# Cross-attention and mixture of experts on one core: the normed queries' rows of batches two to eight are turned on VectorE and placed by DMA instead of transposed on TensorE

## The reference, cut to what matters

```python
def xattn(query, key, value, Wq, Wk, Wv, Wo):      # 16 heads of 16
    q = (query @ Wq.T).reshape(B, L, H, D) * D ** -0.5
    k = (key @ Wk.T).reshape(B, -1, H, D)
    v = (value @ Wv.T).reshape(B, -1, H, D)
    scores = sigmoid(einsum('blhd,bshd->bhls', q, k))
    return einsum('bhls,bshd->blhd', scores, v).reshape(B, L, E) @ Wo.T

x = x + xattn(layernorm(x), ctx, ctx, Wq, Wk, Wv, Wo)
x = x + moe(layernorm(x), gate_w, Wg, Wu, Wd, Ws_g, Ws_u, Ws_d)   # top-64 tokens per expert and batch
```

## Time and profile before

| what | value |
|---|---|
| median of three runs | 1366.16 us |
| the profiled execution | 1361.12 us, of which the span of its instructions is 1359.3 us |
| TensorE matmul busy | 1320.3 us (97%) |
| ScalarE busy | 981.3 us (72%) |
| VectorE busy | 631.8 us (46%) |
| GpSimd busy | 283.5 us (21%) |
| granted TensorE clock, mean | 0.998 |

### The profile page before, as it was taken

How to read it: one execution, slowest core, us unless ns; L and a number is a source line. 1 busy time by engine, 2 the same in 40 slices (tenths; PEclk the granted TensorE clock), 3 DMA queues, 4 the chain that set the end, 5 groups by cost and what they waited for, 6 DMA issues and landing times.

```text
span 1359.3 us, 22554 instructions
## 1 busy us (share of the span) xinstructions
PE 1320.3 (97%) x8834; PEld 755.1 (56%) x8834; DVE 631.8 (46%) x1249; ACT 981.3 (72%) x1137; POOL 283.5 (21%) x286
## 2 busy tenths in 40 slices
PE   4899999999999999999999999999999999999997
PEld 3444344444444444444444443324888888888886
DVE  4353254235226335423522531211658777777762
ACT  3568988888888888888888889997232445555553
POOL 1000020002002002000200200220000466777645
PEclk9999999999999999999999999999999999999999
DMA  6466784587388478458738836833433567877754
GB/s 162 137 142 154 126 161 138 114 143 192 104 138 181 143 116 171 138 115 143 190 104 140 184 105 92 144 126 109 156 124 124 186 191 177 200 191 190 185 109 47
DMA packets 119433, 196.85 MB, mean 145 GB/s; under 512 B 22752, under 2 KB 71904, under 8 KB 119328
## 3 DMA queue, kind: packets, MB, share of 16 engines
q1 hardware_dynamic: 99456, 161.44, 50.0%
q0 software_dynamic: 19584, 33.59, 12.7%
q10 hardware_dynamic: 288, 0.39, 0.2%
HBM read 118.99 MB, written 61.83 MB: 133 GB/s over the span
## 4 chain that ended last, share of the span: by engine, by line
PE 89%; ACT 5%; DVE 2%; issue 1%; SPq 1%; DMA 1%; POOL 0%; POOLq 0%; DVEq 0%; ACTq 0%
PE acc L1420 25%; PE score L1458 19%; PE score L1396 18%; PE score L1476 9%; PE misc L1304 6%; PE misc L1317 6%; ACT probs L735 5%; PE misc L1340 2%; PE misc L1325 2%; SPq L471 1%; PE misc L1332 1%; DMA keys<-key_parts 0%; PE misc L1355 0%; DMA xn<-x 0%; DVE key_parts L851 0%
## 5 line engine op out<-in xcount | busy, mean ns | idle before, releaser
L735 ACT ACTIVATE probs<-score 128x1024 f32<-128x1024 f32 (+1 forms) x832 | 788.6, 1041 | 131.3 <-PE score L1396 125.1
L1420 PE MATMUL acc<-probs,values 128*32 128x512 f32 (+1 forms) x3328 | 412.4, 600 | 1.4 <-ACT probs L735 0.4
L1396 PE MATMUL score<-queries,keys 48*128 48x512 f32 (+1 forms) x1664 | 311.6, 448 | 4.1 <-DMA keys<-key_parts 2.9
L1396 PEld LDWEIGHTS score<-queries,keys 48*128 48x128 f32 (+1 forms) x1664 | 126.7, 180 | 261.1 <-ACT probs L735 200.4
L1420 PEld LDWEIGHTS acc<-probs,values 128*32 128x32 f32 (+1 forms) x3328 | 81.0, 108 | 181.6 <-issue 135.4
L618 POOL DMA_DIRECT2D ctx_raw<-ctx_t x32 | 23.4, 732 | 684.0 <-DVE ctx_lo L840 683.2
L744 ACT ACTIVATE gelu<-score 128x512 f32<-128x512 f32 x96 | 56.6, 599 | 96.5 <-PE score L1458 95.0
L678 POOL DMA_INDIRECT gathered<-norm_scr,gather_row x64 | 80.8, 1262 | 204.5 <-DVE gather_row L1116 189.3
L1458 PE MATMUL score<-tok_hi,gu_hi 128*128 128x512 f32 x384 | 119.2, 391 | 0.0
L1458 PE MATMUL score<-tok_lo,gu_hi 128*128 128x512 f32 x384 | 118.5, 390 | 0.0
L1458 PE MATMUL score<-tok_hi,gu_lo 128*128 128x512 f32 x384 | 118.3, 389 | 0.0
(11 more groups left out here) (185 smaller groups left out, 1430.3 us busy)
## 6 DMA issues: line engine op xcount, KB each, us to landing
keys<-key_scr SPq DMA_DIRECT2D x180, 200.2 KB, 9.2
key_scr<-key_parts SPq DMA_DIRECT2D x45, 512.0 KB, 5.0
gu_raw<-w_gu SPq DMA_DIRECT2D x17, 1024.0 KB
ctx_raw<-ctx_t POOLq DMA_DIRECT2D x24, 512.0 KB, 4.2
queries<-query_scr SPq DMA_DIRECT2D x180, 64.0 KB, 2.8
d_raw<-w_d SPq DMA_DIRECT2D x17, 512.0 KB
query_scr<-query_parts SPq DMA_DIRECT2D x15, 512.0 KB, 4.8
norm<-xn SPq DMA_DIRECT2D x224, 32.0 KB
```

The lines of the kernel that those rows point to most:

```text
L735: act.activation(probs[0:rows, n % RING, 2 * pair:2 * pair + 2, :], score[k % 3][0:rows, :, :], ACT.Sigmoid, scale=SCALE).then_inc(probs_d ...
L1396: mm = pe.matmul(score[k % 3][0:rows, g, :], keys[quarter % KEY_RING][of, pair, P * st:P * st + rows], queries[half][of, e, pair, :], star ...
L1420: mm = pe.matmul(acc[32 * c:32 * (c + 1), :], values[b % 2][0:rows, st, half, c, :], probs[0:rows, n % RING, c, :], start=(st == 0), stop= ...
```

## The change

The T products of batches 1 to 7 go. Their rows take the way of the second norm: `turn_x` (one STREAM_TRANSPOSE of `xn` into `norm_blocks`, at quad 26, in batch 0 at quad 21), `place_x` (16 DMAs of 32 KB on GpSimd's queue, back into the bytes of `xn`), `split_x` (four VectorE instructions at quad 33, in batch 0 at quad 31). Q waits for that split. In batches 1 to 6 of the loop Q(c, 0) is at quad 38 where it was at 31, K(c, 0, 3) and K(c, 1, 3) at 40 and 41 (41 and 43), V(c, 3, 0) at 44 (45); most other products move by a quad or two. Batch 0 of the input keeps its two T products ahead of the loop. SP's load of the x rows of the batch after moves from the second T to Q(c, 0), behind a wait for the split.

The plan of sums follows from the list. Quads of a batch b = 1 to 6, by their number of sums: before 21 with none, 21 with two, 10 with one; after 19, 19 and 14. Batch 0: before 21, 19 and 12; after 22, 20 and 10. Batch 7 has no product but O, O and G in both, O at 5 and 8 where they were at 4 and 7.

```diff
 def beside(b):
     if b == 0:
...
-        at_quad = (13, 14, 16, 18, 19, 21, 23, 25, 26, 28, 30, 32, 33, 35, 37, 39, 40, 42, 44)
+        at_quad = (13, 14, 16, 18, 20, 22, 24, 26, 28, 30, 32, 34, 36, 38, 39, 41, 44)
     else:
-        tasks = {4: ("O", b - 1, 0), 7: ("O", b - 1, 1), 26: ("G", b - 1)}
-        at_quad = (0, 2, 10, 13, 15, 18, 21, 24, 28, 29, 31, 33, 35, 37, 39, 41, 43, 45, 47)
+        tasks = {5: ("O", b - 1, 0), 8: ("O", b - 1, 1), 26: ("G", b - 1)}
+        at_quad = (0, 2, 10, 12, 15, 17, 20, 24, 28, 30, 32, 34, 38, 40, 41, 44, 47)
     if b + 1 < B:
         c = b + 1
         names = [("K", c, 0, 0), ("K", c, 1, 0), ("V", c, 0, 0), ("V", c, 0, 1),
                  ("K", c, 0, 1), ("K", c, 1, 1), ("V", c, 1, 0), ("V", c, 1, 1),
-                 ("T", c, 0), ("T", c, 1), ("Q", c, 0),
-                 ("K", c, 0, 2), ("K", c, 1, 2), ("V", c, 2, 0), ("V", c, 2, 1),
+                 ("K", c, 0, 2), ("K", c, 1, 2), ("V", c, 2, 0), ("V", c, 2, 1), ("Q", c, 0),
                  ("K", c, 0, 3), ("K", c, 1, 3), ("V", c, 3, 0), ("Q", c, 1)]
...
             def load_x(b):
-                sp.wait_ge(misc_copied, COUNT["T", b - 1, KC - 1])
+                if b == 1:
+                    sp.wait_ge(misc_copied, COUNT["T", 0, KC - 1])
+                else:
+                    sp.wait_ge(x_split, b - 1)
                 sp.dma_start(xn[:], x_rows[b]).then_inc(x_in, 16)
...
                         elif task[0] == "Q":
+                            if task[2] == 0 and task[1] + 1 < B:
+                                load_x(task[1] + 1)
                             write_queries(*task[1:])
                             if task[1] and task[2] == 0:
                                 stack_queries(task[1], 0)
-                        elif task[0] == "T" and task[2] == KC - 1 and task[1] + 1 < B:
-                            load_x(task[1] + 1)
...
+            def place_x(b):
+                pool.wait_ge(x_turned, b)
+                place_blocks(x_raw, x_placed)
+
+            for kc in range(NCH):
+                load_ctx(1, kc)
+            place_x(1)
+            for b in range(2, B):
+                load_ctx(b, 0)
+                if b >= 3:
+                    place_x(b - 1)
+                for kc in range(1, NCH):
                     load_ctx(b, kc)
-                if b >= 2:
-                    place_norm(b - 2)
+                place_norm(b - 2)
+            place_x(B - 1)
             place_norm(B - 2)
...
+            def turn_rows(of, turned_one):
+
+                dve.transpose(norm_blocks.rearrange("p j (t q) -> p t j q", q=TURN),
+                              of[:].rearrange("p t (j q) -> p t j q", q=TURN)).then_inc(turned_one, 1)
...
+            def turn_x(b):
+                dve.wait_ge(xn_ready, b + 1)
+                wait_past(dve, nt_stored, STORE * (b - 1))
+                turn_rows(xn, x_turned)
...
+            def split_x(b):
+                dve.wait_ge(x_placed, PLACE_DMAS * b)
+                split_rows(x_raw, x_split)
...
-                    if kind == "T" and k == 0:
-                        wait_past(dve, nt_stored, STORE * (b - 1))
...
-                    if b and q == 7:
+                    if b and q == 8:
                         second_sums(b - 1)
...
+                    if b + 1 < B and q == (21 if b == 0 else 26):
+                        turn_x(b + 1)
+                    if b + 1 < B and q == (31 if b == 0 else 33):
+                        split_x(b + 1)
...
                 elif kind == "Q":
+                    if task[2] == 0:
+                        wait_past(pe, x_split, b)
                     mm = query_product(task[2], bank)
```

More of the change, by code:

```diff
@@ L282, in build @@
         tok_raw = norm[:].rearrange("p t d -> p (t d)").rearrange("p (k s) -> p k s", s=S)
+        x_raw = xn[:].rearrange("p t d -> p (t d)").rearrange("p (k s) -> p k s", s=S)
         last_out = logits[:].rearrange("p t b e -> p (t b e)")[:, 0:P]
@@ L317, in build @@
         norm_ready = sem("norm_ready")
+        x_turned = sem("x_turned")
+        x_placed = sem("x_placed")
+        x_split = sem("x_split")
         norm_turned = sem("norm_turned")
@@ L635, in _, with place_blocks @@
                 load_ctx(0, kc)
+            def place_blocks(to, placed_one):
+                for i in range(BLOCKS):
+                    for j in range(BLOCKS):
+                        pool.dma_start(to[TURN * j:TURN * (j + 1), :, P * i:P * (i + 1)],
+                                       norm_blocks[TURN * i:TURN * (i + 1), j::BLOCKS, :]).then_inc(placed_one, 16)
             def place_norm(b):
@@ L639, in place_norm @@
                 pool.wait_ge(norm_turned, b + 1)
[L640 to L646, removed]
+                place_blocks(tok_raw, norm_placed)
+            def place_x(b):
[9 more added lines that the diff above has]
+                for kc in range(1, NCH):
                     load_ctx(b, kc)
-                if b >= 2:
-                    place_norm(b - 2)
+                place_norm(b - 2)
+            place_x(B - 1)
             place_norm(B - 2)
@@ L954, in second_sums, with split_rows @@
                 norm_sums(resid)
+            def turn_rows(of, turned_one):
+                dve.transpose(norm_blocks.rearrange("p j (t q) -> p t j q", q=TURN),
+                              of[:].rearrange("p t (j q) -> p t j q", q=TURN)).then_inc(turned_one, 1)
             def turn_norm(b):
                 dve.wait_ge(norm_ready, b + 1)
[L958 to L962, removed]
+                turn_rows(norm, norm_turned)
+            def turn_x(b):
+                dve.wait_ge(xn_ready, b + 1)
+                wait_past(dve, nt_stored, STORE * (b - 1))
+                turn_rows(xn, x_turned)
+            def split_rows(placed_raw, split_one):
                 for k in range(KC):
[L964 removed]
+                    raw = placed_raw[:, k, :].rearrange("p (i t q) -> p t i q", i=BLOCKS, q=TURN)
                     hi = nt_hi[:, k, :].rearrange("p (t i q) -> p t i q", i=BLOCKS, q=TURN)
@@ L969, in split_norm @@
                     last = dve.tensor_tensor(lo, raw, hi.bitcast(F32), ALU.subtract)
-                last.then_inc(norm_split, 1)
+                last.then_inc(split_one, 1)
+            def split_norm(b):
+                dve.wait_ge(norm_placed, PLACE_DMAS * (b + 1))
+                split_rows(tok_raw, norm_split)
+            def split_x(b):
+                dve.wait_ge(x_placed, PLACE_DMAS * b)
+                split_rows(x_raw, x_split)
             def gate_logits(b):
```

## The result

The changed kernel takes 1376.11 us, the median of 5 runs (1372.26 to 1377.15). The kernel before took 1366.16 us on the same chip. The ratio is 1.0071, 95% interval 1.0050 to 1.0091: 10 us slower, where 7.5 us faster was forecast. What happened is the second rival, the late keys, with a second cost behind it that no rival had priced: TensorE's clock.

What follows compares the result with a forecast made beforehand. TensorE was taken to bound the kernel, working through its list almost without waiting; 5.9 us from batches 1 to 6 plus 1.6 from batch 0 gave 1366.2 - 7.5 = 1358.7 us, range 1355.5 to 1364.5.

Steps and rivals of the forecast that it cites:

- the second rival: First score of batches 2 to 7: keys land late, costing six times the excess over 0.7 us; 1373 us; chance 0.10.
- The price of the list: TensorE in batches 1 to 6: its quads priced start to start, each batch going from 113.0 to 112.0 us.
- two pairs lost: Sums in batches 1 to 6: two pairs become four singles, losing 0.32 us of the 1.30 gained per batch.
- batch 0: Batch 0: two T products gone, one pair of sums more, a wait behind the second T; 1.6 us gained.
- The first rival: Runs of short quads in each batch: ScalarE takes back up to 0.5 us a batch; 1361.7 us; chance 0.12.
- The placing of x: GpSimd's 16 DMAs after quad 26: landing 3.1 to 8.7 us after issue, 4.4 us of cover at worst; nothing reaches TensorE.
- the third rival: GpSimd's queue, six batches: each of 16 placing DMAs held 1.8 us, 130 us slower; decides from four to five holds; chance 0.02.
- the cost is taken at zero: SP's queue behind the later Q(c, 0): no cost, or 0.3 us a batch if the landing is 1 us later.
- the margin of 0.7 us: Batch end: the sixth key DMA lands 0.7 us before the new quarter starts, where it was 1.5.
- The key writes: SP's queue behind the query stack: small writes taking 0.5 us each to issue and landing in 1.8 us.
- The query write and its stack: SP's queue after quad 38: queries written at 702.7, landed 2.80 us later at 705.5, stacked by 711.0 after 5.4 us.
- A clock under 1.00: TensorE's granted clock: a value under 1.00 was listed among the signs of being wrong, with no size given.

Runs made afterwards that it cites:

- Q at 35: Against the changed kernel, Q(c, 0) moves from quad 38 to 35 and V(c, 2, 1) from 34 to 37; 1361.67 us, ratio 0.9952 to the kernel before.
- the best kernel: Against Q at 35, the small products K(c, 0, 3) and K(c, 1, 3) stand at quads 39 and 41; 1358.58 us, ratio 0.9937 to the kernel before.
- the kernel with the load held back: Against the changed kernel, the load of the third context chunk waits until quad 5 of the next batch; 1363.38 us, ratio 0.9965 to the kernel before.

## Why the prediction was wrong

**What held.** The price of the list: batches of 112.0 us in the changed kernel between its waits; with Q at 35 and the same number of pairs of sums, 112.1 to 112.4 where no clock falls. In the best kernel the two T products less one pair of sums came to 6.65 us over six batches, against 5.9 forecast for two pairs lost (6.8 by the same prices for one), and batch 0 gave 1.8 against 1.6. That the best kernel's gain by the medians is again 7.5 us is in part luck: its list is another one. ScalarE took nothing back: 99.03 us busy in batch 5 against 99.02. The first rival falls with it.

The placing of x held too, with more room than forecast. GpSimd's queue and VectorE in batch 5 of the changed kernel:

```profile
685.24 8.62 POOL L647 DMA_DIRECT2D xn<-norm_blocks  x16 [1.90 <-DVE norm_blocks L978]
...
698.48 0.42 DVE L995 CAST nt_hi<-xn 128x512 fp32r<-128x512 f32 x1
...
700.00 0.69 DVE L997 TENSOR_TENSOR nt_lo<-xn,nt_hi 128x512 fp32r<-128x512 f32 x1
```

The split waits for nothing and is over at 700.69, 8.2 us before Q(c, 0) starts at 708.93. The 16 DMAs land 1.7 to 2.9 us after issue (up to 3.8 in the other batches 1 to 6), not 3.1 to 8.7 as those of the second norm do: the rows used as a bound were dearer than the thing bounded. In batch 0, which the prediction did not walk, they take 8.1 to 12.4 us, and still no product waits for them. Sixteen issues in 8.62 us leave no room for holds like the one in the earlier trace rows, and four of the six batches look like this one. Batches 3 and 6 have one hold each, of 1.7 and 2.4 us; in batch 3 VectorE is idle throughout it, so that not every hold is VectorE's. Two holds in six batches are far from the four or five a batch at which the third rival would decide: it falls.

**What failed** is one step, "the cost is taken at zero", in the part on SP's queue. The mechanism and its place were named there and again in rival 2; its terms were mis-sized, and the margin of 0.7 us was thinner than the sum of their errors. Relative to the nominal start of each batch:

| start of batch | key stack starts before it | sixth has landed after first issue | lateness |
|---|---|---|---|
| forecast | 14.2 | 13.5 | -0.7 |
| 2 | 13.3 | 14.3 | 1.0 |
| 3 | 12.4 | 14.2 | 1.8 |
| 4 | 13.0 | 16.2 | 3.2 |
| 5 | 12.4 | 14.5 | 2.1 |
| 6 | 11.0 | 14.2 | 3.2 |
| 7 | 14.7 | 12.8 | -1.8 |

- The key writes. The prediction used 1.8 us for the landing, from the earlier trace rows, where each write is alone. With both together, right behind twelve reads, the first, for which the key stack waits, takes 2.8 to 3.1: 1.0 to 1.3 us in each batch.
- The query write and its stack. The stack ended up to 0.8 us later than the prediction's sum ahead of batches 2 to 5, and 2.0 later ahead of batch 6, where the write took 4.8 us to land. That this happens is in the trace of before as well: its query write ahead of batch 5 took 4.8 us too. Behind that one's stack stood 12 us without work for SP's queue, so it cost nothing. The prediction knew that such writes exist and held against it that no transfer of size is in flight.
- The context load. V(c, 3, 0) moved from 45 to 44, so its load goes out 11.2 us before the nominal start, not 9.5; and the key stack starts later, so that the load is issued before or among the six key DMAs where it came behind all six (they were issued by 11.9 us before the start). The sixth lands 14.2 to 16.2 us after the first issue, 0.7 to 2.7 above the forecast's 13.5. The prediction followed every step of SP's queue and left out a DMA of another queue that moves by one quad. Batch 7 is the control in the changed kernel itself: no context is loaded ahead of it, the six land in 12.8 us, and it doesn't wait. (Its start, 14.7 us behind the key stack, holds the 1.5 us of the fall at quad 42; without it the keys would be 0.3 us early.)
- The clock. A clock under 1.00 was named as a sign of being wrong, but rival 2 priced a late key at its lateness alone. In the changed kernel waits of 1.0 and 2.1 us were followed by full clock; behind that of 1.8 quad 0 took 3.78, and behind those of 3.2 us quads 0 and 1 took 7.5 instead of 4.8. This made 7.1 us out of nothing in the sum. By rival 2 as written, 11.4 - 7.5 would have been 4 us slower; 10 were measured.

The Trainium skill, page "DMA: Bandwidth & Descriptors", section "Queues, rings and completion order", says that each DMA engine takes turns between the queues that have work for it. The rows agree: a 512 KB load of GpSimd's queue beside 1.2 MB of keys of SP's queue delays the sixth key DMA by 2 us (median 12.2 without it, 14.3 with it), though the key DMAs never wait for it.

**What stands beside the slow query writes.** The write takes 2.8 us in most batches and 4.1 to 5.1 in one batch of each of the ten kernels. The DMA view of the changed kernel from 712.1 to 717 us, where it took 4.85 (queue, packets, MB, share of the 16 engines), has a packet of another kind in it:

```profile
q1 hardware_dynamic: 272, 0.52, 28.7%
q8 instruction: 1, 0.02, 2.2%
```

From 598 to 603 us, where the write took 2.8, there is no `instruction` line. Over all ten traces, 80 query writes land within 6 us of issue. In the ten that take 4.1 us or more, a 16 KB packet of this queue starts 0.9 to 2.0 us after the issue; in none of the other 70 does one start in that stretch. The six keys show something like it. Where no load lies among them, every sixth key DMA that lands more than 12.8 us after the first issue has such a packet among the six, the 13.8 us of the kernel with the load held back and the 13.5 of the earlier trace rows included; but some batches have one and stay at 12.0 to 12.8. No run moved such a packet, so this is a coincidence in every case seen, not a cause that was tested. It says that the forecast's 2.8 us for the query write was a value that one batch of each trace exceeds by 1.3 to 2.3 us.

The falls at quad 42 are narrowed down, not settled.

## What to carry to other kernels

When a product is moved toward the end of a period, walk its transfers to the first instruction of the next period, and count every load of the other queues that falls into the same stretch: a margin under 1 us on such a chain is no margin, since the query write (2.0 us in one batch), the key write (1.0 to 1.3) and the sixth key DMA (0.7 to 2.7) each lost more than that here. Take a DMA's duration from a row with the same neighbours, not from a row where it is alone. And price a wait of TensorE above its length: here 3.2 us of waiting cost 6.0.

## What was not expected of the hardware

- Each of the ten waits of 2.7 us or more at the start of batches 2 to 6, over all profiled kernels, was followed by the lower clock level, with 1.5 to 3.0 us of extra time in quads 0 and 1. Of the shorter ones that of 1.0 us cost only itself, that of 1.8 cost 1.5 more, and of two of 2.1 one was free and one cost 1.5.
- The clock fell to 0.50 without any idle time, behind two neighbouring quads with 66-column products, in 7 of 24 batches; each cost 1.5 to 3.1 us.
- The clock in the first 100 us differs from execution to execution of any of these kernels (0.89 to 1.00 up to the first score group). Batch 1 starts between 160.1 and 166.8 us over the seven kernels with the changed way for x.
- Ten query writes of 512 KB that took 4.1 to 5.1 us, and none of 70 that took 2.8 to 3.7, had a 16 KB packet of the queue for instructions start 0.9 to 2.0 us after their issue.
